# Four due times moved in a hand-ordered five-engine kernel: a copy of the c projection, a copy of the keys, the product for the values, and GpSimd's last two operations on the state c

## The reference

```
A_bar = exp(dt * A);  h = A_bar * h + dt * B * x;  y = sum over 16 states of h * C
y = (y + D * x) * silu(z);  out = y @ c_proj
```

```
f, i = sigmoid(x @ wf + c @ uf + bf), sigmoid(x @ wi + c @ ui + bi);  g = tanh(x @ wc + c @ uc + bc)
c = f * c + i * g;      h = tanh(x @ wo + c_final @ uo + bo)
```

## Time and profile before

| | |
|---|---|
| median of 3 runs | 1267.78 us (1267.23 to 1269.12) |
| the profiled execution | 1265.77 us, span 1264.5 us |
| mean granted TensorE clock | 0.986 of full |
| instructions | 12574 |
| ScalarE busy | 795.0 us, 63% of the span |
| GpSimd busy | 982.6 us, 78% |
| step 0 of half 0 starts at | 97.57 us |
| step 0 of halves 3 and 4 | 527.79 and 671.42 us |

### The profile page before, as it was taken

One profiled execution on the slowest core, in us unless ns is written; L12 is line 12 of the kernel. 1 busy time (PEld: TensorE's weight loads), 2 busy tenths in 40 slices (PEclk: granted clock), 3 DMA queues, 4 the chain that ended last, 5 costly groups with the idle time before them and its releaser, 6 DMA issues.

```text
span 1264.5 us, 12574 instructions
## 1 busy us (share of the span) xinstructions
PE 1140.8 (90%) x3612; PEld 640.1 (51%) x3612; DVE 1155.2 (91%) x1138; ACT 795.0 (63%) x1445; POOL 982.6 (78%) x712
## 2 busy tenths in 40 slices
PE   7989678998999899997999899997999899789996
PEld 5636333664457444764457443763457443444453
DVE  3768999999999999899999999899999999999987
ACT  2256567765786668755786668755786667655532
POOL 3216886889778887989778997889778996976862
PEclk9999989999999999999999999999999999899998
DMA  7308588766868688866878679876868786899922
GB/s 285 115 16 315 176 269 284 278 233 233 281 226 297 200 278 292 289 233 225 290 219 301 197 277 311 276 241 217 292 217 287 215 282 236 290 335 346 374 86 116
DMA packets 92309, 313.87 MB, mean 248 GB/s; under 512 B 10432, under 2 KB 15680, under 8 KB 91984
## 3 DMA queue, kind: packets, MB, share of 16 engines
q1 hardware_dynamic: 89936, 306.26, 70.3%
q10 hardware_dynamic: 2304, 6.82, 1.5%
HBM read 301.73 MB, written 11.31 MB: 248 GB/s over the span
## 4 chain that ended last, share of the span: by engine, by line
PE 43%; DVE 22%; POOL 14%; ACT 9%; issue 8%; DMA 3%; SPq 0%; DVEq 0%; POOLq 0%; ACTq 0%
PE ps L907 13%; DVE ps L1741 12%; POOL arena L1970 8%; PE ps L601 5%; PE ps L830 4%; PE ps L609 3%; DVE arena L1749 3%; DMA arena<-bc_scratch 2%; PE ps L647 2%; PE ps L751 2%; PE ps L723 2%; ACT ps L1295 2%; ACT arena L931 2%; PE ps L728 1%; PE ps L633 1%
## 5 line engine op out<-in xcount | busy, mean ns | idle before, releaser
L1970 POOL TENSOR_TENSOR arena<-arena 128x1024 f32<-128x1024 f32 x255 | 600.3, 2362 | 136.5 <-PE ps L907 113.2
L1741 DVE TENSOR_TENSOR_SCAN ps<-ps,arena 128x1024 f32<-128x1024 f32 (+1 forms) x257 | 585.8, 2280 | 30.3 <-ACT ps L1295 17.9
L907 PE MATMUL ps<-arena,identF 128*128 128x512 f32 x1024 | 482.8, 603 | 49.0 <-DVE arena L1749 29.4
L1295 ACT ACTIVATE ps<-arena,negA 128x512 f32<-128x512 f32 x512 | 332.7, 683 | 83.2 <-DVE arena L1749 78.2
L907 PEld LDWEIGHTS ps<-arena,identF 128*128 128x128 f32 x1024 | 190.3, 193 | 267.2 <-issue 208.8
L1749 DVE TENSOR_TENSOR arena<-ps,arena 128x1024 f32<-128x1024 f32 (+1 forms) x257 | 312.0, 1214 | 5.9
L922 ACT ACTIVATE arena<-arena,rnln 128x256 f32<-128x256 f32 x118 | 61.9, 589 | 42.1 <-POOL rnln L1776 24.9
L647 PE MATMUL ps<-arena,inw 128*128 128x512 f32 x128 | 60.0, 614 | 11.7 <-ACT arena L931 9.6
L1307 ACT ACTIVATE arena<-ps 128x2 f32<-128x2 f32 x128 | 22.0, 172 | 64.9 <-DVE arena L1749 64.4
L931 ACT ACTIVATE arena<-ps,modT 128x512 f32<-128x512 f32 x43 | 51.7, 1266 | 14.7 <-PE ps L474 12.6
L728 PE MATMUL ps<-arena,inw 128*128 128x512 f32 x128 | 60.2, 592 | 0.0
(11 more groups left out here) (222 smaller groups left out, 1707.1 us busy)
## 6 DMA issues: line engine op xcount, KB each, us to landing
arena<-bc_scratch SPq DMA_DIRECT2D x511, 512.0 KB, 5.0
arena<-in_x SPq DMA_DIRECT2D x16, 256.0 KB, 6.9
arena<-in_x SPq DMA_DIRECT2D x8, 512.0 KB, 8.4
xr_scratch<-arena SPq DMA_DIRECT2D x6, 512.0 KB, 6.9
px_scratch<-arena SPq DMA_DIRECT2D x6, 512.0 KB, 6.1
out_x<-arena SPq DMA_DIRECT2D x5, 512.0 KB, 2.6
arena<-bc_scratch SPq DMA_DIRECT2D x9, 256.0 KB, 3.6
woT<-in_woT SPq DMA_DIRECT2D x4, 512.0 KB, 10.0
```

The costliest lines, as they stand in the source:

```text
L907: x = pe.matmul(ps[:, Y, :], identF[:], inp[:, m % RING, q, :], start=False, stop=(i == BLOCK_STEPS - 1 and q == 1), skip_group_check=True)
L1295: x = act.activation(ps[:, 2 * (m % 2) + q, :], dt[:, kd, :], ACT.Exp, scale=negA[:, kd, 2 * i + q:2 * i + q + 1])
L1741: x = dve.tensor_tensor_scan(states, states, inp[:, m % RING, q, :].rearrange("p q t -> p (q t)"), 0.0, ALU.mult, ALU.add)
L1970: x = pool.tensor_tensor(inp[:, m % RING, :, :], u[:, kd:kd + 1, :].broadcast_to([P, 2, TH]), b_at[:, m % 3, :, :], ALU.mult)
```

## The change

Four entries of the table, and one condition so that the last two operations on c of half 6 stay where they were.

- ScalarE's second copy of the c projection: due 5.25 and no longer 5. It is emitted behind the decay that step 5 issues (for step 6) and no longer ahead of it.
- ScalarE's copy of the keys of heads 1 to 3, for halves 2 to 7: due 4.5 and no longer 4.25 of `before`, which is step -0.75 and no longer -1 of the half that runs. It is emitted behind the decay for step 0.
- TensorE's product for the values of head 0, for halves 2 to 7: due 6 and no longer 5.25, which is step 0.75 and no longer 0. It is emitted behind both halves of the sums of step 31, right ahead of the second scores.
- GpSimd's `i_g` and `c_new`, for g up to 5: due 26.25 and 27.25 and no longer both 25.5. `i_g` comes behind input 28 and `c_new` behind input 29; both were between input 27 and input 28.

```
-        "s0": 2, "q1": 2, "k1": 3.75, "v0": 5.25,       (pe_before)
+        "s0": 2, "q1": 2, "k1": 3.75, "v0": 6,
-        "exp0b": 4.25, "k1": 4.25, "v0": 7, ...         (act_before)
+        "exp0b": 4.25, "k1": 4.5, "v0": 7, ...
-    "act_after": {"cp_ev": (2.75, 5), ...
+    "act_after": {"cp_ev": (2.75, 5.25), ...
-    "pool_after": {..., "f_c": 21, "i_g": 25.5, "c_new": 25.5},
+    "pool_after": {..., "f_c": 21, "i_g": 26.25, "c_new": 27.25},
```

```
-            yield t + TIMES["pool_after"]["i_g"]
+            yield t + (25.5 if g == G - 2 else TIMES["pool_after"]["i_g"])
             pool.wait_ge(S.g_sig, 2 * g + 2)
             pool.wait_ge(S.g_ev, 6 * g + 6)
             pool.tensor_tensor(gates["i"], gates["i"], gates["c"], ALU.mult).then_inc(S.i_g, 1)
-            yield t + TIMES["pool_after"]["c_new"]
+            yield t + (25.5 if g == G - 2 else TIMES["pool_after"]["c_new"])
             pool.wait_ge(S.c_f, g + 1)
             pool.wait_ge(S.i_g, g + 1)
             pool.tensor_tensor(c_of(g), gates["f"], gates["i"], ALU.add).then_inc(S.c_new, 1)
```

More of the change, by code:

```diff
@@ L57 @@
     "act_before": {"hn1": (-3.5, -3.5), "hB1": (-2.25, -2.25), "q0": 0, "k0": 0, "q1": 3.25, "exp0a": 4.25,
-        "exp0b": 4.25, "k1": 4.25, "v0": 7, "exp1a": 7, "exp1b": 7, "att0": 9, "v1": 9, "att1": 10.75,
+        "exp0b": 4.25, "k1": 4.5, "v0": 7, "exp1a": 7, "exp1b": 7, "att0": 9, "v1": 9, "att1": 10.75,
         "op_ev": (12, 12.5), "hn2": (14.25, 14.25), "q_scr": 17.5, "xdT": (19.75, 19.75), "ffn_ev": (21.25, 21.25),
@@ L66 @@
         "softplus": (33.75, 33.75), "dt_copy": 41.25, "xc_silu": 28.5},
-    "act_after": {"cp_ev": (2.75, 5), "z_tanh": (5.75, 8, 8.5, 9.25), "hA": (10.25, 10.25),
+    "act_after": {"cp_ev": (2.75, 5.25), "z_tanh": (5.75, 8, 8.5, 9.25), "hA": (10.25, 10.25),
         "gate": (12.25, 15.75, 17.5, 20.25, 22.5, 26), "sigmoid": (11.5, 17.5, 17, 21.5, 22.5, 25.25),
@@ L82 @@
         "ln3_rstd": 22.75, "u": (34.5, 39.25), "cut": (34.5, 42)},
-    "pool_after": {"cp_gate": -7.25, "cp_add": (5, 5), "ln4_rstd": 6.75, "f_c": 21, "i_g": 25.5, "c_new": 25.5},
+    "pool_after": {"cp_gate": -7.25, "cp_add": (5, 5), "ln4_rstd": 6.75, "f_c": 21, "i_g": 26.25, "c_new": 27.25},
 }
```

## The result

The changed kernel took 1277.62 us (median of 6 runs, 1275.3 to 1280.59) against 1268.51 for the kernel before (6 runs, 1267.23 to 1270.34): a ratio of 1.0074, interval 1.0057 to 1.0091. That is 9.1 us slower, where the prediction said 6.4. A second measurement of the same pair gave 1276.03 against 1269.17, a ratio of 1.0059 (1.0044 to 1.0075), 6.9 us. The profiled execution took 1275.3 us, span 1273.8, against 1265.77 and 1264.5.

The account below looks back on a forecast made before the run. TensorE's unbroken queue from step 25 to step 8, then VectorE, was taken to bound the kernel. Terms 0.80 + 3.3 + 0.7 + 1.65 = 6.4 us over the median 1267.78 gave 1274.2 us, range 1267 to 1280.

Parts of the forecast that it names:

- What bounds it: Each period of 32 steps: TensorE's unbroken queue from step 25 to step 8, then VectorE up to the next step 25.
- The two copies, 0 each: Steps 0 and 6: moved copies free the decays, but at step 6 L1462's wait grows from 0.19 to 1.43; net 0.
- The values, +0.80 once: Passage from half 0 to half 1: TensorE stands 1.2 us for product 31, c projection 0.80 us later, once.
- GpSimd's operations can't hasten input 28: Input 28 needs TensorE's sums of step 24, so scan 28's 1.65 us wait stays; scan 29 late by 1.4.
- The other crossings, +1.11 and +0.33: Passages between halves: 1 to 2, 3 to 4, 5 to 6 lose 1.11 us each; 2 to 3, 4 to 5 lose 0.33.
- The walk: Step-by-step timing of passages between halves with measured durations; product 31 2.06 us late in half 3, median 1274.2; chance 0.75.
- The crossing from 6 to 7, +1.65: Passage from half 6 to 7: VectorE sets the time; GpSimd's delay of some 3.4 less 1.66 spare, about 1.65 us late.
- The clock: Rival: TensorE's clock halves behind the three large new gaps, 14 us more, near 1288; chance 0.03.
- The sum: Total over all passages between halves: 0.80 + 3.3 + 0.7 + 1.65 = 6.4 us slower.

Follow-up runs that it names:

- half_values2: Kernel before with half of the values' product of head 0 (8 of 16 matmuls) left out in halves 2 to 7; 1269.02 us, ratio 0.9993.
- copies_only: Kernel before with only ScalarE's two copies (keys, c projection) moved behind the decays; 1268.38 us, ratio 0.9997.
- values_only: Kernel before with only TensorE's product for the values moved behind the sums of step 31; 1270.43 us, ratio 1.0009.
- no_pool: Kernel before with all of the change but GpSimd's i_g and c_new, which stay ahead of input 28; 1270.26 us, ratio 1.0008.
- tiny_state2: Kernel before with i_g and c_new computed on one column of each 512, in their old place; 1269.04 us, ratio 1.0002.
- filler_after2: Changed kernel plus two zero-adding matmuls of 512 columns before L736 of step 11; 1275.25 us, ratio 1.0051 to the kernel before.
- pool_only: Kernel before with only GpSimd's i_g and c_new moved, to 26.25 and 27.25; 1273.27 us, ratio 1.0031.

## Why the prediction was right or wrong

- **What bounds it.** Right, and shown from both sides: 0.9 us less in TensorE's queue is 0.80 to 0.92 less per crossing (`half_values2`), a wait of 0.85 us put into it is 1.1 more (the changed kernel), and VectorE's waits taken away are worth nothing (`copies_only`).
- **The two copies, 0 each.** Right in sign and place. The wait of L1462 in half 4 was to grow by 1.24 and grew by 1.35.
- **The values, +0.80 once.** Right: 0.78 or 0.79 in the profiles of the changed kernel, `values_only` and `no_pool`.
- **GpSimd's operations can't hasten input 28.** Right: `tiny_state2`. Scan 29's wait was to be 1.4 and is 1.34.
- **The other crossings, +1.11 and +0.33.** Right to 0.02. The walk put product 31 2.06 us late in half 3, and it is 2.06 late (676.67 against 670.80, less the 3.81 that came in).
- **The crossing from 6 to 7, +1.65.** This step failed, and in size, not in mechanism. The walk took 1.66 us of GpSimd's slack from the earlier trace rows. In that one profile L751 of half 6 had run at half speed for most of its time (3.64 us for eight matmuls) ahead of the sums that input 28 waits for, and so GpSimd was 1.55 us later than with a fast one. In the changed kernel's profile L751 takes 2.24, input 28 starts 1.55 earlier by the recurrence's time, and the slack is 1.66 + 1.55 = 3.2 for a delay of 3.4, so some 0.2 was due and 0.09 came. `filler_after2`, where L751 took 3.17, has the 1.68 that was forecast. Of the ten profiles in which L751 stands in this place it is fast in six and slow in four. I took for the kernel's a row that differs from one execution to the next. (The prediction also says, of its signs, that half 7 should start 1.4 late; that doesn't fit its own 1.65, and neither came.)
- **The clock.** The rival named a mechanism that exists and put it in the wrong place. Behind the new gaps the granted clock stayed 1.00, in windows of 7 to 11 us over all six crossings up to half 6. It fell at step 11 of halves 2 and 4, behind gaps that the kernel before has too (1.37 us before L736), and cost 1.7 us each, 3.4 and not 14. The Trainium skill, page "TensorE: Matmul & The Clock Gate", part 1, says that the block which watches TensorE's activity runs free and doesn't start anew with the kernel, so that the moment at which the clock changes depends on where the work falls in its time. The traces agree as far as they reach: after the same 1.37 us of standing, L736 of half 2 took 3.56 to 3.67 us where it started at 436.61, 436.74 or 436.93, and 1.98 or 1.99 where it started at 435.24, 435.93 or 437.36. In half 4, though, it took 3.00 at 726.18 and 1.98 at 726.26. What decides it stays open.
- **The sum.** 4.8 us of crossings in the profiles against 4.8 forecast for the same six; 0.1 for 1.65; 3.4 and 1.1 of clock that were not in it, the 1.1 none of the change's. The measured 9.1 and 6.9 us differ by more than any term, and runs of one kernel spread over 5 us. That 6.9 lies so near the 6.4 is luck: a term of 1.65 stayed away, and half-speed stretches that the sum didn't have came in its place. Nor do the profiles show what a middling run loses, since the two profiled executions, 1275.3 and 1274.74, are the fastest and the second fastest of their six.

Parts add up as far as can be told: 4.4 for `pool_only` and 1.4 for `no_pool` are 5.8; what the five crossings cost more when both are there (0.2 at each odd one, 0.1 at the two even ones together) makes 0.8, which gives 6.6. The 1.4 isn't clear of noise, so this is a check of size and no more.

No version here beats the kernel before. What shortens a crossing is less work in TensorE's queue between step 25 and step 8, and the one way tried of moving work out of it lengthened the chain into it.

## What to carry to other kernels

A wait is worth removing only if the next wait on that engine doesn't take it up: find the instruction behind it that another engine's unbroken queue pins, and price the wait at nothing up to there. Work that stands in a forced wait is free, even if that wait is named after its engine. Moved out, it costs what the new place can't hide: here 4.8 us of GpSimd's work made product 31 up to 2.1 us late, and a crossing 0.3 or 1.1. Where a term is the difference of two slacks, look at the clock of the stretch that the slack comes from, in more than one half or profile.

## What the hardware showed that I had not expected

TensorE's half-speed stretches can come back in the same place. In both profiles of the changed kernel they hit the same four matmuls, step 11 of halves 2 and 4, for 1.7 us each. In profiles of other orders of work they stand elsewhere: with the values alone in halves 1 and 2 (1.10 and 1.70), with GpSimd's move alone in half 3 (1.1), in `half_values2` in half 6 (1.7), with the filler at L751 of half 6. Each of these is one profile, so it isn't shown whether the order or the execution decides. Their price is that of the place: at L751 in the profile of before 1.4 us of half speed cost nothing, since VectorE had slack there. So edits that save 0.9 us five times over can leave the median where it was.
